# Masked cross-attention on one Trainium2 core: the mask added by TensorE instead of VectorE

## The reference, cut to what matters

```python
q = _split_heads(query @ wq_k + wq_b, H)
k = _split_heads(key_in @ wk_k + wk_b, H)
v = _split_heads(value @ wv_k + wv_b, H)
logits = jnp.einsum('bhqd,bhkd->bhqk', q, k) / jnp.sqrt(jnp.asarray(dh, q.dtype))
neg = (1.0 - mask.astype(q.dtype)) * -1000000000.0
logits = logits + neg[:, None, :, :]
attn = jax.nn.softmax(logits, axis=-1)
attn = attn * group_prob[:, None, :, :]
out = jnp.einsum('bhqk,bhkd->bhqd', attn, v)
out = out.transpose(0, 2, 1, 3).reshape(query.shape[0], -1, H * dh)
return out @ wo_k + wo_b
```

## Time and profile before

| | |
|---|---|
| median of 3 runs | 6137.96 us |
| the profiled execution | 6125.29 us, its span 6123.2 us |
| busy over the span | PE 4198.8 us (69%), DVE 4473.8 us (73%), ACT 2776.4 us (45%), POOL 3058.1 us (50%) |
| the masked cross-attention | from about 2614 to 3308 us |
| TensorE's granted clock | mean 0.824 of full speed |

### The profile page before, as it was taken

One profiled execution on the slowest core, in us unless ns is written; L12 is line 12 of the kernel. 1 busy time (PEld: TensorE's weight loads), 2 busy tenths in 40 slices (PEclk: granted clock), 3 DMA queues, 4 the chain that ended last, 5 costly groups with the idle time before them and its releaser, 6 DMA issues. The chain is left out here.

```text
span 6123.2 us, 104442 instructions
## 1 busy us (share of the span) xinstructions
PE 4198.8 (69%) x29561; PEld 2419.5 (40%) x29564; DVE 4473.8 (73%) x8773; ACT 2776.4 (45%) x6405; POOL 3058.1 (50%) x3374
## 2 busy tenths in 40 slices
PE   5777777777777777657775777745456767577743
PEld 2333233323333333335553555545444555355521
DVE  6999999999999999867786555542455655444468
ACT  3555555555555555446663333345533433233334
POOL 6877777777777777645554221244511121222202
PEclk8888898988899899878786888867778888788865
DMA  2111111111111111044443444441244443444420
GB/s 74 59 61 61 61 61 61 61 58 50 44 60 61 61 61 61 33 78 83 87 82 58 85 86 84 91 132 54 84 81 77 73 77 65 79 76 77 76 49 28
DMA packets 319765, 420.49 MB, mean 69 GB/s; under 512 B 39955, under 2 KB 301286, under 8 KB 308710
## 3 DMA queue, kind: packets, MB, share of 16 engines
q1 hardware_dynamic: 315110, 408.16, 28.4%
q0 software_dynamic: 4352, 8.95, 0.4%
HBM read 307.46 MB, written 109.58 MB: 68 GB/s over the span
## 5 line engine op out<-in xcount | busy, mean ns | idle before, releaser
L2163 POOL TENSOR_TENSOR m_h<-m_dtu,m_Bb 128x512 f32<-128x512 f32 x1024 | 1585.7, 1577 | 237.6 <-PE bank L1798 231.5
L1798 PE MATMUL bank<-m_h,ident 128*128 128x512 f32 x2048 | 1216.6, 686 | 496.1 <-DVE m_h L2062 484.2
L1798 PEld LDWEIGHTS bank<-m_h,ident 128*128 128x128 f32 x2048 | 364.3, 207 | 1160.8 <-DVE m_h L2062 1010.0
L2056 DVE TENSOR_TENSOR_SCAN m_h<-m_dA,m_h 128x512 f32<-128x512 f32 x512 | 756.0, 1477 | 6.2 <-DVE m_sz L1989 5.9
L2062 DVE TENSOR_TENSOR m_h<-m_h,bank 128x512 f32<-128x512 f32 x1024 | 672.6, 657 | 4.8 <-DVE m_h L2056 2.7
L2056 DVE TENSOR_TENSOR_SCAN m_h<-bank,m_h 128x512 f32<-128x512 f32 x512 | 620.6, 1212 | 28.1 <-DVE m_sz L1989 11.7
L1945 ACT ACTIVATE bank<-m_dt,m_A 128x512 f32<-128x512 f32 x512 | 352.3, 688 | 491.7 <-DVE m_h L2056 432.5
L1945 ACT ACTIVATE m_dA<-m_dt,m_A 128x512 f32<-128x512 f32 x512 | 367.2, 717 | 432.6 <-DVE m_h L2056 428.8
L510 ACT ACTIVATE x_sm<-x_sm,x_nm 128x77 f32<-128x77 f32 x1024 | 353.3, 348 | 117.4 <-DVE x_nm L672 117.3
L674 DVE TENSOR_REDUCE f_nm<-bank 128x4 f32<-128x512 f32 x256 | 176.3, 689 | 256.5 <-PE bank L342 254.8
L342 PE MATMUL bank<-x_Ks,x_Qs 128*128 128x77 bf16 x2048 | 175.2, 215 | 252.7 <-DMA x_Ks<-x_k_parts 213.3
(11 more groups left out here) (424 smaller groups left out, 10852.7 us busy)
## 6 DMA issues: line engine op xcount, KB each, us to landing
m_Bb<-m_B SPq DMA_DIRECT2D x32, 4096.0 KB, 12.0
x_Ks<-x_k_parts SPq DMA_DIRECT2D x32, 462.0 KB
x_q_parts<-x_qp SPq DMA_DIRECT2D x32, 384.0 KB, 2.5
x_Qs<-x_q_parts SPq DMA_DIRECT2D x32, 384.0 KB
f_Ks<-f_k_parts SPq DMA_DIRECT2D x16, 768.0 KB
a_Ks<-a_k_parts SPq DMA_DIRECT2D x16, 768.0 KB
x_xp<-x_stage SPq DMA_DIRECT2D x32, 256.0 KB
x_Qs<-x_q_parts SPq DMA_DIRECT2D x32, 256.0 KB
```

What stands on the lines that cost most here:

```text
L1798: pe.matmul(banks[4 + c], ident[:], h[:, k % RING, :], start=(s == 0), stop=(s == NS - 1)).then_inc(s_ya.sem, 1)
L2056: v.tensor_tensor_scan(h[:, k % RING, :], decays[k % AHEAD], h[:, k % RING, :], 0.0, ALU.mult, ALU.add).then_inc(s_h.sem, 1)
L2163: pool.tensor_tensor(h[:, k % RING, :], dtu[:, d, c, :], Bb[:, d, s, :], ALU.mult).then_inc(s_dB.sem, 1)
```

## The change

The mask becomes a bf16 tile `hidden`, 125 where a position is masked and 0 elsewhere, made by VectorE at step 1 as before. `hide` holds two 128x128 diagonals in bf16, -61 x 2^17 and -9 x 2^9, built once by GpSimd at the start of the stage. In every step of this stage TensorE first runs two products of `hide` with the mask tile, repeated over the four heads (308 columns each), into the bank; 125 x (61 x 2^17 + 9 x 2^9) is 1e9. The four score products accumulate on top. VectorE takes the maxima from PSUM, with no add and no copy to `sm`. ScalarE's exponentials read PSUM and write `sm`. A bank is free again when the exponentials (`s_e`) have read it, where it was free after VectorE's add (`s_Sf`). ScalarE, and no longer VectorE, waits for the old contents of `sm` to be used (`s_tw`), once per sample. The other three attention stages keep their code but for the name of a semaphore.

```diff
@@ attention
-        neg = sb("neg", [P, 2, GB, S2]) if mask is not None else None
+        hidden = sb("hidden", [P, 2, GB, S2], BF16) if mask is not None else None
+        hide = sb("hide", [P, 2, P], BF16) if mask is not None else None
...
+        s_read = s_Sf if gate is None else s_e
@@ scores (TensorE)
                 if c == 0 and q == 0:
                     pe.wait_ge(s_stk.sem, s_stk.at(2 * i + l + 1))
-                pe.wait_ge(s_Sf.sem, s_Sf.at(b, c + 1 - 2))
+                    if mask is not None:
+                        pe.wait_ge(s_neg.sem, s_neg.at(2 * i + l + 1))
+                pe.wait_ge(s_read.sem, s_read.at(b, c + 1 - 2))
+                if mask is not None:
+                    o = bankS[c % 2][:, 0:4 * sk].rearrange("p (h k) -> p h k", h=4)
+                    for part in range(2):
+                        pe.matmul(o, hide[:, part, :], hidden[:, l, q, :].unsqueeze(1).to_broadcast([P, 4, S2]),
+                                  start=(part == 0), stop=False)
                 for h in range(4):
                     hh = 4 * c + h
                     ins = pe.matmul(bankS[c % 2][:, h * sk:(h + 1) * sk], Qs[:, l, hh, q * S:(q + 1) * S],
-                                    Ks[:, l, hh, q * sk:(q + 1) * sk], start=True, stop=True)
+                                    Ks[:, l, hh, q * sk:(q + 1) * sk], start=(mask is None), stop=(mask is None or h == 3))
...
@@ exp_rows (ScalarE)
                 act.wait_ge(s_mx.sem, s_mx.at(b, c + 1))
                 act.sem_inc(s_step, 1)
+                if c == 0:
+                    act.wait_ge(s_tw.sem, s_tw.at(b - 1))
+                    act.sem_inc(s_step, 1)
                 for h in range(4 * c, 4 * c + 4):
-                    ins = act.activation(sm[:, lm % 2, h, :], sm[:, lm % 2, h, :], ACT.Exp, bias=nm[:, lm % 2, 0, h:h + 1],
+                    ins = act.activation(sm[:, lm % 2, h, :], bankS[c % 2][:, (h - 4 * c) * S2:(h - 4 * c + 1) * S2], ACT.Exp, bias=nm[:, lm % 2, 0, h:h + 1],
...
@@ masks (VectorE)
-                v.wait_ge(s_Sf.sem, s_Sf.at((g - 1) * GB))
-                v.tensor_scalar(neg[:, par], mi[:], 1.0, 1e9, ALU.subtract, ALU.mult).then_inc(s_neg.sem, 1)
+                v.wait_ge(s_S.sem, s_S.at((g - 1) * GB))
+                v.tensor_scalar(hidden[:, par], mi[:], 1.0, -MASK[0], ALU.subtract, ALU.mult).then_inc(s_neg.sem, 1)
@@ maximum (VectorE)
-                if mask is not None:
-                    hs = slice(4 * c, 4 * c + 4)
-                    if c == 0:
-                        v.wait_ge(s_tw.sem, s_tw.at(b - 1))
-                    v.tensor_tensor(sm[:, p, hs, :], src, neg[:, l, q, :].unsqueeze(1).to_broadcast([P, 4, S2]),
-                                    ALU.add).then_inc(s_Sf.sem, 1)
-                    v.wait_ge(s_Sf.sem, s_Sf.at(b, c + 1))
-                    v.tensor_reduce(nm[:, p, 0, hs], sm[:, p, hs, :], AX.X, ALU.max, negate=True).then_inc(s_mx.sem, 1)
-                else:
-                    v.tensor_reduce(nm[:, p, 0, 4 * c:4 * c + 4], src, AX.X, ALU.max, negate=True).then_inc(s_Sf.sem, 1)
+                ready = s_Sf if mask is None else s_mx
+                v.tensor_reduce(nm[:, p, 0, 4 * c:4 * c + 4], src, AX.X, ALU.max, negate=True).then_inc(ready.sem, 1)
@@ setup (GpSimd), for each of the two parts
+                    pool.memset(hide[:, part, :], 0.0).then_inc(s_pool, 1)
+                    pool.wait_ge(s_pool, n + 1)
+                    pool.affine_select(out=hide[:, part, :], in_=hide[:, part, :], compare_op=ALU.not_equal, fill=-MASK[1 + part], base=0,
+                                       pattern=[[-1, P]], channel_multiplier=1).then_inc(s_pool, 1)
```

More of the change, by code:

```diff
@@ L21 @@
 EPS = 1e-5
+MASK = (125.0, 61.0 * 2 ** 17, 9.0 * 2 ** 9)
 class Count:
@@ L447, in _ @@
             pe.wait_ge(s_zero.sem, NZ)
+            if mask is not None:
+                pe.wait_ge(s_setup.sem, 1)
             turn(0, first=True)
@@ L792, in _ @@
                 n += 1
+            if mask is not None:
+                for part in range(2):
+                    pool.wait_ge(s_pool, n)
+                    pool.memset(hide[:, part, :], 0.0).then_inc(s_pool, 1)
+                    pool.wait_ge(s_pool, n + 1)
+                    pool.affine_select(out=hide[:, part, :], in_=hide[:, part, :], compare_op=ALU.not_equal, fill=-MASK[1 + part], base=0,
+                                       pattern=[[-1, P]], channel_multiplier=1).then_inc(s_pool, 1)
+                    n += 2
             pool.wait_ge(s_pool, n)
```

## The result

The changed kernel takes 6161.60 us (median of 9 runs, 6155.4 to 6170.55), the kernel before 6136.15 in 9 runs beside it (6115.85 to 6142.14). The profiled execution has 6161.6 us and a span of 6159.7, against 6123.2 before.

The account below looks back on a forecast made before the run. Each group was taken as bound by a TensorE/VectorE front plus a DMA chain. Ten fronts at +1.10, five at -0.30, group 15 -5 and setup +0.5 gave +5 us: 6130 profiled, 6143 median, range 6110 to 6172.

Parts of the forecast that it names:

- the bank paces: Rival: waiting for the scores' bank makes every step from 3 on 1.63 instead of 1.32 us; 6171 us, chance 0.25.
- same: Sign of the result: time within about 0.2%, 12 us, of the kernel before; chance 0.39.
- What bounds the group: Masked stage: front (first scores to K store) plus chain (store, reload, landing); TensorE's wait for Ks grows to 6 to 7 us.
- Mask products: TensorE, two products per step: 0.27 us at full clock, 0.51 at low; +0.64 up to step 3, +1.33 in steps 3 to 7.
- The bank behind the evacuation: Scores wait for exponentials that stand behind ScalarE's copy: +0.64 us at slot 2, +0.35 at slot 4, 0.99 per front.
- The exponential from PSUM: ScalarE, priced at copies out of a bank: 0.326 us at 77 columns against 0.348 from SBUF; four with readout 1.44.
- VectorE's relief: 16 adds per group removed, VectorE busy down by 128 us; worth at most 1.34 us per front, nothing at its end.
- Group 15: Last group, no successor, 15 steps paced by VectorE in 33.3 us: 28.3 after the change, -5 us.
- The chain moves nothing: Store, reload and landing of the K tile keep the same DMAs in the same SyncE order: no change.
- The stop at a turn: ScalarE's standstill of some 8 us where groups 4, 6, 8, 10, 12 begin a loop turn: mostly hidden, -0.30 us each.
- VectorE didn't pace: Denies the rival that the front follows VectorE and falls by 1.9 us: 6105 us, chance 0.22.
- the products didn't cost double: Denies the rival of mask products 0.27 us dearer per step at full clock, +2.8 per group: 6185 us, chance 0.05.

Follow-up runs that it names:

- e3: The changed kernel without the two mask products on TensorE, the mask left out of the scores: 6137.02 us, ratio 1.0023 to the kernel before.
- e6: The changed kernel with one fill of 3072 columns, about 2.6 us, at the end of VectorE's loop body: 6155.93 us, ratio 1.0062 to the kernel before.
- e5: The changed kernel with a one-column fill on VectorE after each maximum, restoring its old number of instructions: 6144.52 us, ratio 1.0042 to the kernel before.

## Why the prediction was right, and where it failed

The measured median, 6161.60, is 19 us above the 6143 of the forecast. It lies inside the whole range (6110 to 6172), but above the forecast's own (6131 to 6157), 9 us below what the rival "the bank paces" gave (6171). The sign, slower by more than 0.2%, had 0.38, and "same" one hundredth more.

- *What bounds the group.* Held: front and chain, and TensorE's wait for Ks grew (89.6 us in 12, 7.5 each; forecast 6 to 7). The two waits "booked on the weight load" before are two of the 13, not more.
- *Mask products.* Held: 0.28 and 0.48 us for two, forecast 0.27 and 0.51; step 3 at 8.24, forecast 8.14. In e3 all of them are worth 1.76 per undisturbed front in the mean (2.32 in group 5), forecast 1.97.
- *The bank behind the evacuation.* Held: step 4 at 10.32, forecast 10.28, with the wait on L525 in the row. Two small errors cancel in it: step 3 came 0.10 later, and the four exponentials with the last readout took 1.33 us and not 1.44 (the prediction's own rows, 3 x 0.326 + 0.52, give 1.50). Step 8 at 19.95 and the front of 23.53 are the forecast (19.95 and 23.50). The mean of the nine undisturbed fronts rose by 0.75, less than 1.10, and by 1.24 with the loop written out.
- *The exponential from PSUM.* Its row is 331 ns, forecast 326, and 17 less than before; its readout took 211 ns against 189. But the two overlap, and what ScalarE needs for a step is the distance from one exponential's start to the next: 342 ns before and 300 after, in the median of the stage, and 1.48 and 1.34 us for four with the last readout. So an exponential from PSUM gained 42 ns, where the prediction took 22. The Trainium skill (VectorE: DVE Perf Modes, the section on the TRN2 errata) had 43 ns less than from SBUF. The trace agrees with it. Step 2 of group 5, before and after, and the rows after:

```profile
2857.96 0.35 ACT L510 ACTIVATE x_sm<-x_sm,x_nm 128x77 f32<-128x77 f32 x1
...
2858.30 0.35 ACT L510 ACTIVATE x_sm<-x_sm,x_nm 128x77 f32<-128x77 f32 x1
```
```profile
2869.50 0.32 ACT L525 ACTIVATE x_sm<-bank,x_nm 128x77 f32<-128x77 f32 x1
...
2869.80 0.33 ACT L525 ACTIVATE x_sm<-bank,x_nm 128x77 f32<-128x77 f32 x1
```
```profile
L525 ACT ACTIVATE x_sm<-bank,x_nm 128x77 f32<-128x77 f32 x768 | 239.4, 331 | 85.5 <-DVE x_nm L681 83.5
L525 ACT ACTIVATION_READ_ACCUMULATOR x_sm<-bank,x_nm 128x1 f32 x768 | 162.3, 211 | 0.0
```

- *VectorE's relief.* 107 us on the page, forecast 128. The 256 adds alone were 121 us; the cast of the middle K part now takes 0.80 us instead of 0.41, which takes 6 of them back. It moves nothing: from the maximum of step 7 to the last K part it is 4.53 us, forecast 4.52.
- *Group 15.* Held: 15 steps in 28.6 us, forecast 28.3, and -5.7 to the stage's end, forecast -5. Setup and group 0 cost 3.2, forecast 1.6.
- *The chain moves nothing.* It rose by 0.2 each, +3.1. Open.
- *The stop at a turn.* **This step failed**: "I take the stop as mostly hidden", -0.30 in five groups. I reasoned that an engine that reaches the end of the body earlier is held earlier. For ScalarE the end of the stop did come earlier, at 1.5 us into the group in the mean of five against 2.5 before. For VectorE e6 refutes the reason: the end of the stop is tied to the start of the turn, not to the arrival. And I had asked what ScalarE's stop would do, never whether a shorter body could give VectorE one. That is the +22.8 us of the table in place of -1.5, and it is nearly all of the 25 by which the stage missed its +5. Of the 22.8 us, e5 gives 15.8 back by taking VectorE's stop away.

The rivals: the bank didn't pace, as TensorE's waits on the exponentials are 10.0 us in 29 of 193 steps (53 if the weight load's are counted), not in most; VectorE didn't pace, as the store came at 23.5 and not before 22; and the products didn't cost double. What moved the time most was a mechanism that none of them had, so that 6161.60 lies near "the bank paces" is chance. So the forecast was near by its own steps for the undisturbed groups; for the whole it was near by luck, as a miss of 25 us in one stage is small beside 6140.

## What to carry to other kernels

Moving work off a full engine pays only where that engine sets the period. Here a group was bound by a front on TensorE and a chain of DMAs; with the loop written out, the same change cost 20 us of its stage in one schedule and gained 5 in another, whose preparation came early enough to make VectorE the bound. So first remove the wait that ends last, then ask again what an edit is worth. And where a kernel is a loop of long bodies, look for rows "<- issue" at the turns and for the packets of the instruction queues before and after an edit: the number of instructions in a body can cost more than their durations.

## What was unexpected of the hardware

- Removing 16 adds and their waits per group from VectorE's loop body added a stop of some 10 us of VectorE at each turn; with 16 fills of one column per group it no longer holds up the maxima (fronts of the turns 28.2 and 25.0 us).
- A stop ends at a set moment of the turn, even if the engine arrives 3 us later (e6).
- Writing out one stage's loop made a later, unchanged stage 19 to 28 us slower (691.7 to 700.0 us against 672.4); with that one written out too it was 21 faster again.
- An exponential that reads PSUM follows the one before after 300 ns, one that reads SBUF after 342, though their rows differ by only 17.
- Products of the mask tile repeated over the four heads run at the rate of plain bf16 columns: 616 columns in 0.28 us at full clock.
